# Every second product q*k of an attention kernel computed by GpSimd instead of VectorE

## What is computed

```python
q = (x @ Wq + bq).reshape(B, T, 16, 64)
kv = ((x @ Wdown + bdown) @ Wup + bup).reshape(B, T, 16, 128)
k, v = jnp.split(kv, 2, axis=-1)                  # rotated by the token's place, q and k alike
att = softmax(einsum('bthd,btgd->bthg', q, k) / 8)
x = layernorm(x + einsum('bthg,btgd->bthd', att, v).reshape(B, T, 1024) @ Wout + bout)
h = silu(x @ wg.T / 127) * (x @ wu.T / 127)       # 3072 hidden columns
x = layernorm(x + h @ wd.T / 127)
```

## Time and profile before

| | us |
|---|---|
| time, median of 2 runs | 3644.08 (3604.76 and 3683.39) |
| the profiled execution, its own time | 3600.2 |
| its slowest core, the one the page shows | 3598.4 |
| its fastest core | 3559.5 |

### The profile page before, as it was taken

The page is one execution under the profiler, slowest core; times in us unless marked ns, Lnnn a source line. Parts: engine busy times, 40 slices in busy tenths (PEclk is TensorE's granted clock), DMA queues, the critical chain, the costliest instruction groups (busy, mean ns, idle before and its releaser), DMA issues.

```text
span 3598.4 us, 42099 instructions; the slowest of 8 cores (3559.5 to 3598.4 us)
## 1 busy us (share of the span) xinstructions
PE 2719.1 (76%) x12672; PEld 1083.2 (30%) x12672; DVE 1674.9 (47%) x2454; ACT 819.5 (23%) x1479; POOL 292.4 (8%) x540
## 2 busy tenths in 40 slices
PE   0000686879887989798978997898889887989566
PEld 0000212233333333333333433333333333333222
DVE  1221345455546544563546364645464446554302
ACT  0000311133214220413041403240234123321101
POOL 0111000001100110011001100010001000110110
PEclk9999856699999999999999999999999998999678
DMA  6887200212332232222231223123322322222222
GB/s 179 242 239 206 48 1 24 42 38 65 91 77 79 65 94 71 79 59 88 65 100 48 80 83 109 40 61 92 94 65 62 92 61 76 65 91 62 90 77 80
DMA packets 108705, 303.97 MB, mean 84 GB/s; under 512 B 16192, under 2 KB 24768, under 8 KB 108496
## 3 DMA queue, kind: packets, MB, share of 16 engines
q1 hardware_dynamic: 61520, 169.14, 16.6%
q0 software_dynamic: 46976, 132.15, 12.5%
HBM read 269.77 MB, written 39.85 MB: 86 GB/s over the span
## 4 chain that ended last, share of the span: by engine, by line
PE 60%; DMA 10%; DVE 8%; issue 6%; ACT 5%; DVEq 0%; ACTq 0%; POOLq 0%; POOL 0%; SPq 0%
PE P L448 10%; PE P L733 9%; PE P L405 9%; PE P L395 9%; PE P L749 7%; PE P L644 7%; DMA wgb<-wg_s 3%; DVE p_sb L696 3%; PE P L585 3%; DMA wub<-wu_s 3%; PE P L344 2%; DMA wqb<-wq_s 2%; PE P L787 2%; DVE esum L670 2%; DMA wob<-wout_s 2%
## 5 line engine op out<-in xcount | busy, mean ns | idle before, releaser
L696 DVE TENSOR_TENSOR p_sb<-P,vdup 128x512 bf16<-128x512 f32 x1024 | 700.0, 690 | 462.6 <-PE P L749 330.5
L395 PE MATMUL P<-x_bf,wgb 128*128 128x512 bf16 x1536 | 513.7, 402 | 110.6 <-DMA wub<-wu_s 90.0
L405 PE MATMUL P<-x_bf,wub 128*128 128x512 bf16 x1536 | 515.4, 400 | 15.7 <-DVE h_sb L421 15.6
L749 PE MATMUL P<-p_sb,id_sb 128*128 128x256 bf16 x2048 | 487.5, 293 | 37.0 <-DVE p_sb L696 31.2
L448 PE MATMUL P<-h_sb,wdb 128*128 128x512 bf16 x1536 | 498.1, 389 | 12.2 <-DVE r_bf L457 11.0
L733 PE MATMUL P<-e_sb,selz_sb 16*128 16x512 bf16 x1024 | 420.1, 416 | 92.1 <-DVE e_sb L680 55.8
L619 DVE TENSOR_TENSOR hadb<-q_sb,krep 128x2048 bf16<-128x2048 bf16 x256 | 309.3, 1224 | 324.6 <-PE P L644 231.0
L644 PE MATMUL P<-hadb,selred_sb 128*16 128x256 bf16 x2048 | 327.2, 278 | 47.3 <-ACT e_sb L631 25.7
L311 PE MATMUL P<-x_bf,wd_sb 128*128 128x512 bf16 x128 | 35.1, 422 | 359.9 <-DMA x_bf<-xt 359.7
L421 DVE TENSOR_TENSOR h_sb<-s_sil,P 128x512 bf16<-128x512 bf16 x192 | 130.9, 682 | 354.5 <-PE P L405 287.5
L701 ACT ACTIVATE avn<-P 128x256 bf16<-128x256 f32 x128 | 49.2, 384 | 987.5 <-PE P L749 981.8
(11 more groups left out here) (69 smaller groups left out, 1940.7 us busy)
## 6 DMA issues: line engine op xcount, KB each, us to landing
wdb<-wdn_s SPq DMA_DIRECT2D x64, 768.0 KB, 4.5
wgb<-wg_s POOLq DMA_DIRECT2D x192, 256.0 KB, 3.0
wub<-wu_s POOLq DMA_DIRECT2D x192, 256.0 KB, 3.0
wob<-wout_s SPq DMA_DIRECT2D x128, 256.0 KB, 3.1
wqb<-wq_s SPq DMA_DIRECT2D x64, 256.0 KB, 3.0
yt<-x2b SPq DMA_DIRECT2D x64, 256.0 KB, 2.0
stg<-wg SPq DMA_DIRECT2D x24, 512.0 KB, 5.3
stg<-wu SPq DMA_DIRECT2D x24, 512.0 KB, 5.3
```

The costliest lines, as they stand in the source:

```text
L395: e.matmul(o, l, r, start=st, stop=sp)),
L405: e.matmul(o, l, r, start=st, stop=sp)),
L696: add('V', (lambda e, o=o, a=a, b=b: e.tensor_mul(o, a, b)), waits=w, inc=s_v, d=640)
L749: e.matmul(o, id_sb[:, :], r, start=st, stop=sp)),
```

## The change

The multiplications of even g stay on VectorE; those of odd g, 128 of the 256, go to GpSimd's queue ('G'), in the attention's chain, with a cost of 2900 in the scheduler where VectorE's is 1460. They count on a semaphore of their own, `s_gv`; the matmuls of odd g wait for it, and so does the first write of the next slice's queries. Buffers, their number, the operation and its operands stay the same.

```diff
                 for g in range(NH):
-                    w = list(wV([]))
+                    w = list(wV([])) if g % 2 == 0 else []
                     w.append((s_s, kv_evac_g[g]))
 ...
-                    add('V', (lambda e, o=o, a=q3, b=b: e.tensor_mul(o, a, b)),
-                        waits=tuple(w), inc=s_v, d=1460)
-                had_last = s_v.c
+                    if g % 2 == 0:
+                        add('V', (lambda e, o=o, a=q3, b=b: e.tensor_mul(o, a, b)),
+                            waits=tuple(w), inc=s_v, d=1460)
+                    else:
+                        add('G', (lambda e, o=o, a=q3, b=b: e.tensor_mul(o, a, b)),
+                            waits=tuple(w), inc=s_gv, d=2900)
+                had_last = (s_v.c, s_gv.c)
 ...
                         if J == 0:
-                            w.append((s_v, v0 + g + 1))
+                            if g % 2 == 0:
+                                w.append((s_v, v0 + g // 2 + 1))
+                            else:
+                                w.append((s_gv, gv0 + g // 2 + 1))
 ...
-                    w.append((s_v, ck['had_end']))
+                    w.append((s_v, ck['had_end'][0]))
+                    w.append((s_gv, ck['had_end'][1]))
```

More of the change, by code:

```diff
@@ L135, in build_nc @@
         s_s = Sem(ctx, nc, "s_s")
+        s_gv = Sem(ctx, nc, "s_gv")
         s_pe2 = Sem(ctx, nc, "s_pe2")
@@ L239, in build_nc @@
                     (s_ld + s_ld2 + s_x + s_gd + s_st + s_out +
-                     [s_pe, s_v, s_s, s_pe2, s_v2, s_s2])}
+                     [s_pe, s_v, s_s, s_gv, s_pe2, s_v2, s_s2])}
         OPS = {k: [] for k in "TVSYG"}
@@ L606, in plan_sc @@
                 h0 = hf * HF
-                pe0, v0, sc0 = s_pe.c, s_v.c, s_s.c
+                pe0, v0, gv0, sc0 = s_pe.c, s_v.c, s_gv.c, s_s.c
                 q3 = q_sb[0:128, 0:XC * ST].rearrange("p (J t) -> p J t", J=XC)[:, :, h0:h0 + HF]
                 for g in range(NH):
-                    w = list(wV([]))
+                    w = list(wV([])) if g % 2 == 0 else []
                     w.append((s_s, kv_evac_g[g]))
@@ L997, in build_nc @@
         all_sems = (s_ld + s_ld2 + s_x + s_gd + s_st + s_out +
-                    [s_pe, s_v, s_s, s_pe2, s_v2, s_s2])
+                    [s_pe, s_v, s_s, s_gv, s_pe2, s_v2, s_s2])
         cnt = {id(sm): SEM_BASE[id(sm)] for sm in all_sems}
```

## The result

The changed kernel takes 3962.65 us in the median, against 3605.14 for the kernel before in the same sessions. The ratio is 1.100, with an interval of 1.096 to 1.104, which is 361 us of 3605. Both medians hold some executions in which the cores of one die ran at a lower clock and took longer; every ratio here compares only those without it. The profiled execution has a slowest core of 3960.4 us, where 3598.4 stood. The forecast was 3950 (3740 to 4160).

A forecast was written before the change was run, and what follows sets the result against it. VectorE's pace and the product buffer were taken to bound first-half score stages, TensorE's order the second-half ones. 219 + 122 - 63 + 48 = +326 on 3600 gave 3926; the median was forecast as 3950 (3740 to 4160).

The forecast's parts named there:

- slice of 418 us: Whole slice: the profiled 374.7 us was forecast to become about 418.
- T: GpSimd's time for one odd multiplication in the score stages, taken as 4.7 us: two passes at VectorE's element pace.
- First half: First-half score stages and slice 0's second: a pair takes 6.1 us instead of 2.62, +24.3 a stage, +219 in all.
- rival C: TensorE's clock falls in first-half score stages: 3980 to 4040 us; slice 0 likely sees it (+12). Chance 0.10.
- Second half: Second-half score stages of slices 1 to 7: a pair takes 7.6 us instead of 5.14, +122 in all.
- Moved matmuls, -63: Up to 42 feed-forward matmuls a slice move into first-half scores, free there, and save their columns' time elsewhere: -63 us.
- GpSimd's DMAs, +48: Score stages of slices 1 to 7: two DMA issues per feed-forward tile always count, waits for wgb are covered; +48 us.
- VectorE's saving at nothing: Score stages: VectorE loses 156 us of busy time, costed at nothing.
- rival B: VectorE's multiplication can't run beside GpSimd's; second-half scores delay product L421: +97, 4023 us. Chance 0.12.

The follow-up runs named there:

- split_after: Changed kernel with a semaphore of its own for the wub load, so GpSimd issues it right behind wgb without waiting for that to land; ratio 1.065.
- order_dve: Changed kernel's order on TensorE, ScalarE and the DMA queues, but the 128 odd multiplications run in VectorE's queue; ratio 1.0265 to the kernel before.
- d1460: Changed kernel with the scheduler's cost of GpSimd's multiplication set to 1460 in place of 2900; ratio 1.098 to the kernel before.
- the control: Kernel before with a semaphore of its own for the wub load, so it is issued right behind wgb; ratio 0.982.
- four_buf: Changed kernel with two product buffers for each engine instead of one, in slice 0 alone; a pair there takes 4.99 us.
- memset3: Changed kernel with each odd multiplication replaced by three constant writes on GpSimd that read nothing, 4.16 us together; ratio 1.086 to the kernel before.

## Why the prediction was right, and where it was not

The direction, its cause (the odd buffer's chain) and its size came out: +326 on the profiled execution forecast (3926), +362 measured (3960.4). That the forecast of the median, 3950, lies nearer still to 3962.65 is luck: its last 24 us came from the spread of two runs of the kernel before. The slice of 418 us was a slip, as its own terms give 374.7 + 24.3 + 17.4 - 9.0 + 6.9 = 414; measured were 423.0. And several terms were wrong, in opposite ways.

**T.** Taken as 4.7, measured 4.05. Two passes at VectorE's element pace was the wrong picture, as the pace is 1.89 ns an element and not 2.18; the value was near. The slope that it is multiplied by was right (112 forecast, 114 and 116 measured). Too much: 0.65 x 112 = 73 us. The Trainium skill's figure for 2048 fp32 elements (GPSIMD Engine Reference, Performance versus the Vector engine) was closer than mine from rows.

**First half.** With T at 4.05 the step gives 5.44 a pair and +19.7 a stage; measured 5.5 and +18.2 in slices 1 to 6. In slice 0, +23.8 and +23.3: in most of its pairs the matmuls run at the low clock (eight in 1.87 us at 0.50), and those pairs are 6.3, as rival C said of that slice.

**Second half.** With T at 4.05, (4.05 + 2.93 - 5.14) x 7 = +12.9 a stage; measured +16.0, with pairs of 7.5 in the mean where 7.6 was forecast. The missing 3 match the 3.0 a slice for which GpSimd's multiplications stand behind a DMA issue; in split_after that is 1.2 a slice, and the stage 4.2 shorter.

**Moved matmuls, -63: this step failed.** The plan did as said (31 more in scores 1, where 42 was the bound), but nothing was gained where they left. The step took their columns' time as saved. order_dve shows +95 for this order when VectorE multiplies, and d1460 no difference when GpSimd does. What stands in its place is the clock: the value stage without them falls to 0.50 for its first 40 us, and with them gone from scores 1 it is that stage whose clock falls. I had the clock as a rival with the wrong place: I feared for it in the first-half scores, where the moved matmuls held it at 0.92, and not where they had left. The 5.9 us of "between" in order_dve go with a lower clock (0.89 against 0.98) and 2.0 us more of waiting for `wob`; what brings these about stays open.

**GpSimd's DMAs, +48.** split_after gives 125 in all against 66 for the control, so 59 (25 to 94 by the intervals): the size came out, but by luck, as the reason was wrong. I had said that the issues always count and the wait for wgb is covered. The issues cost nothing in the first halves, where they fit into the wait for the eight matmuls, and it is the late wub that holds the chain in the second.

**VectorE's saving at nothing** was right and too kind: rival B is true. Its price was forecast at 97 for the product L421 in the second half; it is about 64 (37 to 91), and in other places, the layer norm and the sums. The pairs hide it, as the even multiplication fits beside the eight matmuls either way. The Trainium skill states the exclusion (SBUF — State Buffer, Who interferes with whom), and that a GpSimd instruction that only writes isn't part of it; four_buf (4.99 a pair) and memset3 (1.225 for all 128) agree with both.

So the sum: 326 - 73 for T, + 63 for the matmuls, + about 64 for the exclusion gives 380, where 361 was measured; 19 us are less than the 64 is uncertain by. The forecast was nearer than its parts, and that is luck: too long a T stood in for an exclusion I had left out.

## What to carry to other kernels

Before half of a chain's links go to a slower engine, work out the chain of one buffer with the slower link in it: here 4.05 + 1.39 against 2.62 decides everything, and the idle share of either engine says nothing. Ask next what the two engines share, and look for it outside the stage too, where the slow instruction runs ahead of its time. And where VectorE seemed to need help, a third buffer gave what a second engine couldn't: a ratio of 0.969 with the split semaphore, against 0.982 with that semaphore alone. The pace was set by the buffer, not by the engine.

## What the runs showed of the hardware

- An instruction that is held by the other engine is recorded as busy, on both sides (5.03 and 5.07 us for 4.05 and 1.22). A group whose mean is far above its shortest, 2551 against 1210 ns, is how a page of the profile shows it; the time of waiting is not idle time there. The engine that began first is not slowed (4.05).
- A constant of 128x2048 takes GpSimd 1.80 us, a multiplication of two bf16 operands of that size 4.05.
- Filling work can hold TensorE's clock, so work taken from a stage may cost that stage as much as it frees: 27 matmuls in 10 us at 0.50 against 44 at 1.00.
- A DMA issue of 0.59 us in GpSimd's queue is free where GpSimd would wait anyway (0.15 to 0.16 us from the last matmul to the next multiplication with it or without), and holds the work behind it where it is itself released late (1.16 us).
- VectorE's recorded 1.22 us is 1.14 us of pace when nothing stands between two multiplications.
